# Attention with a mixture-of-experts layer: an early product for values and logits, a third subtraction on ScalarE, and paired score and value steps

## The reference

```python
xn = layernorm(x)                      # x: (8, 512, 128), float32
# attention, 16 heads of 8 channels
q, k, v = split(xn @ w_attn)           # w_attn: (128, 384)
mask = causal - log1p(softplus(decay)[h] * log1p(distance))
att = softmax(q @ k.T / sqrt(8) + mask)
attn = (att @ v) @ w_proj
# mixture of 8 experts, hidden 512, the best two by router logits
logits = xn @ Wr.T
gate = weights of the top 2 of softmax(logits), normalised
ffn = sum over the two of gate * (W2[e] @ silu(W1[e] @ xn))
out = x + attn + ffn
```

## Time and profile before

| | us |
|---|---|
| median of three runs | 574.65 (573.76 to 575.19) |
| the profiled execution | 580.15 |
| its span | 578.4 |
| PE busy | 517.7 (90%) |
| POOL busy | 371.5 (64%) |
| DVE busy | 352.7 (61%) |
| ACT busy | 320.7 (55%) |

### The profile page before, as it was taken

The page is one execution under the profiler, slowest core; times in us unless marked ns, Lnnn a source line. Parts: engine busy times, 40 slices in busy tenths (PEclk is TensorE's granted clock), DMA queues, the critical chain, the costliest instruction groups (busy, mean ns, idle before and its releaser), DMA issues.

```text
span 578.4 us, 13697 instructions
## 1 busy us (share of the span) xinstructions
PE 517.7 (90%) x4472; PEld 370.1 (64%) x4472; DVE 352.7 (61%) x1418; ACT 320.7 (55%) x569; POOL 371.5 (64%) x610
## 2 busy tenths in 40 slices
PE   3589999999999989999999989989999999999930
PEld 1477565565555555565555555545699999999930
DVE  5875898779866766776776676666133333333326
ACT  3656776767776666766776677556523333233300
POOL 3354576467787888788678888888245455554434
PEclk9757999999999999999999999999999999999975
DMA  6553673331430350350241243044546666766439
GB/s 164 164 176 104 189 153 110 111 103 46 134 89 15 121 159 15 98 174 20 83 143 46 70 126 105 16 148 117 134 135 203 210 194 203 221 197 202 145 122 326
DMA packets 69715, 76.49 MB, mean 132 GB/s; under 512 B 8318, under 2 KB 52352, under 8 KB 69648
## 3 DMA queue, kind: packets, MB, share of 16 engines
q1 hardware_dynamic: 65328, 67.16, 39.7%
q0 software_dynamic: 4320, 8.47, 4.3%
HBM read 46.16 MB, written 29.89 MB: 131 GB/s over the span
## 4 chain that ended last, share of the span: by engine, by line
PE 69%; POOL 15%; DVE 6%; issue 3%; DMA 3%; ACT 1%; SPq 1%; another core or an unknown queue 0%; DVEq 0%; POOLq 0%
PE psT L1176 20%; PE ps L1224 11%; PE psT L1251 11%; PE psO L1190 10%; POOL scores L671 8%; POOL rows_dram L682 7%; PE ps L1152 6%; DVE scores L1013 3%; PE psM L1129 3%; PE psM L1082 2%; PE psO L1101 2%; PE psM L1208 1%; DVE x_all L489 1%; PE ps L1215 1%; PE psM L1135 1%
## 5 line engine op out<-in xcount | busy, mean ns | idle before, releaser
L1013 DVE CUSTOM_DVE_ANT_0 scores<-ps,wdist 128x256 f32<-128x256 f32 (+3 forms) x512 | 222.2, 486 | 92.1 <-PE ps L1152 66.3
L671 POOL TENSOR_SCALAR scores<-scores,row_max 128x384 f32<-128x384 f32 (+2 forms) x448 | 221.5, 509 | 77.2 <-DVE row_max L1013 76.0
L776 ACT ACTIVATE probs<-psT 128x512 f32<-128x512 f32 x320 | 175.5, 596 | 80.8 <-PE psT L1176 78.5
L1176 PE MATMUL psT<-ident,scores 128*128 128x128 f32 x1280 | 179.3, 282 | 16.8 <-POOL scores L671 10.9
L1176 PEld LDWEIGHTS psT<-ident,scores 128*128 128x128 f32 x1280 | 138.3, 142 | 57.0 <-POOL scores L671 28.3
L689 POOL DMA_INDIRECT picked_dram<-scores,row_ring x71 | 69.7, 982 | 79.1 <-issue 42.9
L1190 PE MATMUL psO<-probs,values 128*32 128x512 f32 (+3 forms) x1024 | 94.9, 444 | 0.0
L794 ACT ACTIVATE scores<-ps 128x512 f32<-128x512 f32 x71 | 42.4, 597 | 94.1 <-PE ps L1224 94.1
L1224 PE MATMUL ps<-scores,wdist 128*128 128x128 f32 x568 | 75.2, 275 | 1.6 <-issue 1.0
L1251 PE MATMUL psT<-wdist,scores 128*128 x568 | 75.2, 275 | 0.3 <-ACT scores L794 0.3
L682 POOL DMA_INDIRECT rows_dram<-xn_all x64 | 62.8, 981 | 16.2 <-issue 16.2
(11 more groups left out here) (130 smaller groups left out, 322.9 us busy)
## 6 DMA issues: line engine op xcount, KB each, us to landing
wdist<-w1t SPq DMA_DIRECT2D x71, 256.0 KB
k_rows<-k_dram SPq DMA_DIRECT2D x64, 96.0 KB, 3.0
q_rows<-q_dram SPq DMA_DIRECT2D x64, 96.0 KB, 2.5
row_ring<-rows_dram SPq DMA_DIRECT2D x71, 65.0 KB
probs<-picked_dram SPq DMA_DIRECT2D x8, 512.0 KB, 6.8
rows_dram<-row_ring SPq DMA_DIRECT2D x7, 585.0 KB, 5.4
k_dram<-k_parts SPq DMA_DIRECT2D x8, 384.0 KB
q_dram<-q_parts SPq DMA_DIRECT2D x8, 384.0 KB
```

Of the source, the lines that this page charges most:

```text
L671: last = nc.gpsimd.tensor_scalar(part, part, -1.0, row_max[:, r, tile, quad:quad + 1], ALU.mult, ALU.add)
L776: nc.scalar.activation(probs[:, at.ring(2), w, :], psT[:, w % 2], ACT.Exp, scale=-1.0).then_inc(exp_ready, 1)
L1013: last = nc.vector.tensor_tensor_reduce(out=scores[:, r, u, col:col + n], in0=bank[:, col:col + n], in1=wdist[:, at.g * QUADS + quad, SEQ ...
L1176: last = nc.tensor.transpose(psT[:, w % 2, place * P:(place + 1) * P], scores[:, at.ring(2), u, col + key * P:col + (key + 1) * P], ident[:])
```

## The change

The values product and the logits product become one, 136 columns wide (`VL`), for every batch in the prologue and slots 0 and 1. Its result goes half through `psO` and ACT, half through `psM` and DVE, into a staging place; POOL copies the logits out of it (`LC`), SP stores the values of batches 1 to 7 to DRAM (`VS`) and reads them back once per batch (`VR`), and ACT spreads them into `values` (`V`). Unit 6 is subtracted by ACT instead of POOL. In a slot P1 0 and 1, P1 2 and 3, PV 0 and 1, and PV 2 and 3 stand next to each other. The sends stand behind P1 4 and start in slot 8 instead of 10; routing takes slots 2 to 8 instead of 2 to 9 (its last two steps stay in 11 and 12). The normalising of batches 1 to 3 goes to POOL (`NP`), the statistics of the last four batches are split into four steps, the first batch's key and query parts are written for 32 of 128 rows first, and PE gets 18 and 16 matmuls of the identity with itself in the prologue (`WU`).

```diff
@@ -71,24 +71,25 @@
 P1_TILES = (((0, 3),), ((0, 2), (384, 0)), ((0, 1), (256, 1)), ((0, 3),), ((0, 2), (384, 0)))
 DVE_BATCHES, POOL_BATCHES = (0, 1, 3, 4, 6, 7), (2, 5)
 
-ROUTE = {2: {0: ("R1",), 3: ("R2",)},
-         3: {0: ("R3",), 3: ("R4",)},
-         4: {0: ("R5",), 3: ("R6",)},
-         5: {0: ("R7", "GX"), 3: ("R8",)},
-         6: {0: ("CT",), 3: ("R9",)},
-         7: {0: ("R10",), 3: ("R11",)},
-         8: {0: ("R12",), 3: ("R13",)},
-         9: {0: ("R14",), 3: ("R15",)},
+ROUTE = {2: {0: ("R1",), 1: ("R2",), 3: ("R3",)},
+         3: {0: ("R4",), 1: ("R5",), 3: ("R6",)},
+         4: {0: ("R7", "GX"), 1: ("CT",), 3: ("R8",)},
+         5: {0: ("R9",), 3: ("R10",)},
+         6: {0: ("R11",), 3: ("R12",)},
+         7: {0: ("R13",), 3: ("R14",)},
+         8: {0: ("R15",)},
          11: {0: ("R16",)},
          12: {0: ("R17",)}}
-FIRST_SEND_SLOT = 10
+FIRST_SEND_SLOT = 8
 ALL_UNITS = UNITS * NGROUP
 TOPK = 2
-EARLY = {1: (("XB", 8), ("XS", 8), ("XB", 12), ("XS", 12), ("LN", 8), ("LN", 9), ("NX", 16)),
-         2: (("XB", 16), ("XS", 16), ("LG", 8), ("LN", 10), ("LN", 11), ("CZ", 2), ("NX", 20)),
-         3: (("XB", 20), ("XS", 20), ("LG", 12), ("LN", 12), ("LN", 13), ("NX", 24)),
-         4: (("XB", 24), ("XS", 24), ("LG", 16), ("LN", 14), ("LN", 15), ("CZ", 3), ("NX", 28))}
-EARLY_1 = (("XB", 28), ("XS", 28), ("LG", 20), ("LG", 24), ("LG", 28))
+EARLY = {0: (("VL", 12), ("LN", 4), ("LN", 5)),
+         1: (("NX", 16), ("VS", 12), ("LC", 4), ("LN", 6), ("LN", 7), ("CZ", 1)),
+         2: (("XB", 16), ("XS", 16), ("NX", 20), ("LC", 8), ("LN", 8), ("LN", 9)),
+         3: (("VL", 16), ("XB", 20), ("XS", 20), ("VS", 16), ("NX", 24), ("LC", 12), ("LN", 10), ("LN", 11), ("CZ", 2)),
+         4: (("VL", 20), ("XB", 24), ("XS", 24), ("VS", 20), ("NX", 28), ("LC", 16), ("LN", 12), ("LN", 13))}
+EARLY_1 = (("VL", 24), ("XB", 28), ("XS", 28), ("VS", 24), ("LC", 20), ("LN", 14), ("LN", 15), ("CZ", 3), ("VL", 28),
+           ("VS", 28), ("LC", 24), ("LC", 28))
 SENDS = 3
 SECOND_PICK_SLOT = FIRST_SEND_SLOT + -(-NTILE // SENDS)
 
@@ -99,10 +100,13 @@
 TOKEN_ROW = 1 + ROW
 NOWHERE = 1 << 20
 
+WIDE = C + EXPERTS
+POOL_NORMS = (1, 2, 3)
 NORM_PARTS = (slice(0, TILES), slice(TILES, 4 * TILES), slice(4 * TILES, NTILE))
 VCOL = HD + 1
 VROW = HEADS * VCOL + QROWS - VCOL + 1
-ACT_UNITS = 2
+ACT_UNITS = (0, 1, 6)
+POOL_UNITS = tuple(u for u in range(UNITS) if u not in ACT_UNITS)
 FILLS = 8
 PICKS_STEP, GAP_STEP = 12, 13
 TWO23 = 8388608.0
@@ -159,18 +163,19 @@
     step("KD", n + 1, NGROUP)
     step("QD", n + 1, NGROUP)
     p1(0)
+    p1(1)
     step("TE", n - 1, NGROUP, 0, 2)
     per_batch("KA", -3)
     per_batch("QA", -2)
+    per_batch("VR", -2)
     per_batch("V", -1)
     per_batch("YT", 8)
-    step("SA", n, NGROUP)
+    step("SA", n, NGROUP, (0, 1))
     step("PV", n - 2, NGROUP, 0)
-    p1(1)
+    step("PV", n - 2, NGROUP, 1)
     per_batch("KR", -3)
     per_batch("QR", -2)
     step("TE", n - 1, NGROUP, 2, 4)
-    step("PV", n - 2, NGROUP, 1)
     per_batch("KM", -3)
     per_batch("QM", -2)
     if n == NGROUP + 4:
@@ -183,25 +188,26 @@
                 steps.append(("MU", 0, s + 1))
     if n == SECOND_PICK_SLOT:
         steps.append(("SR", 0))
-    pick = int(n > SECOND_PICK_SLOT)
-    first = SENDS * (n - (SECOND_PICK_SLOT + 1 if pick else FIRST_SEND_SLOT))
-    if 0 <= first < NTILE:
-        steps.append(("SC", 0, pick, first, min(NTILE, first + SENDS)))
     if n < FILLS:
         steps.append(("FL", 0, n))
     p1(2)
+    p1(3)
     step("TE", n - 1, NGROUP, 4, 6)
-    step("PV", n - 2, NGROUP, 2)
     per_batch("KL", -3)
     per_batch("QL", -2)
-    p1(3)
+    step("PV", n - 2, NGROUP, 2)
+    step("PV", n - 2, NGROUP, 3)
     step("TE", n - 1, NGROUP, 6, 8)
-    step("PV", n - 2, NGROUP, 3)
     per_batch("KW", -3)
     per_batch("QW", -2)
     per_batch("XT", -4)
     p1(4)
     step("TE", n - 1, NGROUP, 8, 10)
+    step("SA", n, NGROUP, (6,))
+    pick = int(n > SECOND_PICK_SLOT)
+    first = SENDS * (n - (SECOND_PICK_SLOT + 1 if pick else FIRST_SEND_SLOT))
+    if 0 <= first < NTILE:
+        steps.append(("SC", 0, pick, first, min(NTILE, first + SENDS)))
     if n == NGROUP + 2:
         steps.append(("MU", 0, 0))
     step("NT", n - 3, NGROUP)
@@ -213,13 +219,15 @@
 
 
 PROLOGUE = [
-    ("BN", 0, 0), ("RS", 0, 0), ("NX", 0), ("XB", 0), ("KA", 0), ("QA", 0),
-    ("BN", 0, 1), ("RS", 0, 1),
-    ("KR", 0), ("QR", 0), ("KM", 0), ("QM", 0), ("LN", 0), ("LN", 1), ("LN", 2), ("LN", 3), ("CZ", 0),
-    ("KL", 0), ("QL", 0), ("KW", 0), ("QW", 0), ("KD", 0), ("QD", 0),
-    ("NX", 4), ("NX", 8), ("NX", 12), ("BN", 0, 2), ("RS", 0, 2),
-    ("V", 0), ("XB", 4), ("LG", 0), ("LG", 4), ("LN", 4), ("LN", 5), ("LN", 6), ("LN", 7), ("CZ", 1)]
-MISC_KINDS = ("KA", "QA", "V", "NT", "YT", "PJ", "CT")
+    ("BN", 0, 0, 0, 4), ("RS", 0, 0), ("NX", 0), ("WU", 18), ("XB", 0), ("KA", 0), ("QA", 0), ("WU", 16),
+    ("BN", 0, 1, 4, 16), ("RS", 0, 1), ("NP", 4), ("NP", 8), ("NP", 12),
+    ("KR", 0), ("QR", 0), ("KM", 0), ("QM", 0), ("LN", 0), ("LN", 1),
+    ("KL", 0), ("QL", 0), ("KW", 0, 0), ("QW", 0, 0), ("KD", 0), ("QD", 0), ("KW", 0, 1), ("QW", 0, 1),
+    ("VL", 0), ("XB", 4), ("LN", 2), ("LN", 3), ("CZ", 0),
...
 
+        def v_stage(b):
+
+            flat = (probs[:, 0].rearrange("p u k -> p (u k)")[:, b * TILES * WIDE:(b + 1) * TILES * WIDE] if b < 6 else
+                    o_rows[:].rearrange("p r k -> p (r k)")[:, 0:TILES * WIDE] if b == 6 else
+                    y[:].rearrange("p r t c -> p (r t c)")[:, 0:TILES * WIDE])
+            return flat.rearrange("p (t k) -> p t k", k=WIDE)
+
...
+                def values_store(at):
+                    b = at.c // GROUPS
+                    wait_staged(sp, b)
+                    sp.dma_start(v_dram[b - 1], v_stage(b).rearrange("p t k -> p (t k)")
+                                 ).then_inc(v_stored[max(0, b - 5)], 16)
+
+                def values_load(at):
+                    if at.c == GROUPS:
+                        wait_v_stored(sp, True)
+                    else:
+                        sp.wait_ge(values_ready, at.batches(1))
+                    sp.dma_start(v_back[:].rearrange("p t k -> p (t k)"),
+                                 v_dram[bass.ds(at.batches(1, -1), 1)].rearrange("b p s -> p (b s)")
+                                 ).then_inc(v_loaded, 16)
...
 
+                def normalise_step(at):
+                    b = at.c // GROUPS
+                    pool.wait_ge(rstd_ready, 2)
+                    for t in range(b * TILES, (b + 1) * TILES):
+                        last = nc.gpsimd.tensor_scalar(xn_all[:, t, 3:], x_all[:, t, :], mean[:, t:t + 1],
+                                                       rstd[:, t:t + 1], ALU.subtract, ALU.mult)
+                    last.then_inc(xn_pool, 1)
+
+                def logits_step(at):
+                    b = at.c // GROUPS
+                    wait_staged(pool, b)
+                    nc.gpsimd.tensor_copy(logits[:].rearrange("p (t e) -> p t e", e=EXPERTS)[:, b * TILES:(b + 1) * TILES, :],
+                                          v_stage(b)[:, :, C:]).then_inc(logits_ready, 1)
+
                 def causal_step(at):
...
-                        return
                     r = at.ring(2)
                     for strip in range(2):
                         u = 2 * i + strip
+                        if u in ACT_UNITS:
+                            continue
...
-                        nc.scalar.activation(logits[:], psO[:, 0:NTILE * EXPERTS], ACT.Copy).then_inc(logits_ready, 1)
+                def wide_copy(at):
+
+                    act.wait_ge(misc_full, at.misc("VL", 1))
+                    nc.scalar.activation(v_stage(at.c // GROUPS)[:, 0:2, :],
+                                         psO[:, 0:2 * WIDE].rearrange("p (t k) -> p t k", k=WIDE), ACT.Copy
+                                         ).then_inc(vo_free, 1)
+
...
-                def less_act_step(at):
+                def less_act_step(at, units):
 
                     r = at.ring(2)
-                    for u in range(ACT_UNITS):
+                    for u in units:
                         act.wait_ge(p1_free, at.groups(UNITS, u + 1))
-                        part = scores[:, r, u, :]
-                        nc.scalar.activation(part, part, ACT.Identity, scale=-1.0, bias=row_max[:, r, TILES - 1, u:u + 1]
-                                             ).then_inc(less_act, 1)
-
...
 
                 def v_step(at):
-                    act.wait_ge(misc_full, at.misc("V", 1))
+                    act.wait_ge(v_loaded, at.batches(16))
+                    act.wait_ge(pv_full, at.groups(1, -GROUPS))
                     nc.scalar.activation(value_cols[:, at.parity, :, :, 0:HD],
-                                         psM[:].rearrange("p (t h d) -> p t h d", t=TILES, h=HEADS),
-                                         ACT.Copy).then_inc(misc_free, 1)
```

(42 more changed lines are left out.)

127 lines of the change are left out of this document (89 added, 38 removed), and 3 rows, old and new, of the table PROLOGUE.

## The result

The median after is 538.99 us (four runs, 538.42 to 540.09), against 574.37 (573.76 to 575.19) of the kernel before in the same job. The ratio is 0.9385, with a 95% interval of 0.9366 to 0.9405: 35.4 us faster. The forecast was 536.3. The profiled execution took 539.08 us, with a span of 537.4 and a mean granted clock of 0.98.

A forecast was written before the change was run, and what follows sets the result against it. PE was taken as the bound, busy 90% of the span, with POOL closing the loop in sending slots. Gains of 32.0 (slots 9 to 32), 1.3 (2 to 8) and 5.0 (start) sum to 38.3 us: median 536.3, range 528 to 548.

The forecast's parts named there:

- Fewer runs: All slots: joining two score pairs and two value pairs saves 0.50 us a slot, a plain slot becoming 9.38 us.
- the feared wait of the second score step: Each slot: the second score step might wait for DVE to free step 4's banks, with a margin of 0.2 us.
- rivals C and D: Slots wait for DVE through the pairing: C 16 us back, 552, chance 0.08; D 43 us back, 579, chance 0.03.
- 0.50 less 0.15 for near misses: Each slot: 0.50 us saved by joints, 0.15 charged for small waits on DVE or ACT, ends 0 and 0.6.
- The values product: Slots 3, 7, ... 27: V leaves PE's chain, 0.89 us seven times, 6.2 us.
- Sends: Slots 9 to 32: sends at the slot's end, 0.7 us less POOL work; stage 246.0 us, gain 32.0 in all.
- rival A: Sending slots stay bound by POOL and DVE: 13 us come back, 549 us; chance 0.13.
- More important is what waits for the sends: Sending slots: only the next slot's first subtraction waits for moved sends, 2 us or more to spare, so sending waits go.
- Routing brought forward: Slots 2 to 8: three routing parts crowd DVE in slots 2, 3 and 5, 5.5 us of waits; net gain 1.3.
- Prologue: Start, slots 0 and 1: first turn pair near 42, slot 2 near 51 instead of 56.02; gain 5 us, ends 0 and 8.
- the gaps of slot 0: Slot 0: PE's long gaps would drop the clock again after the added matmuls; half clock counted in slots 0 and 1.
- I carry the difference over unchanged: Whole kernel: the profiled execution's 5.5 us over the median (580.15 against 574.65) was taken to stay after the change.

The follow-up runs named there:

- u_unpaired: The changed kernel with score steps and value chunks apart again, in the order of the kernel before: 549.61 us, ratio 0.958.
- p_both: The kernel before with score steps and value chunks in pairs and the sends at the slot's end: 557.66 us, ratio 0.972.
- c_before: The kernel before, unedited, profiled again: 573.60 us, ratio 0.999.
- p_sends: The kernel before with only the sends moved behind the last score step of their slot: 564.02 us, ratio 0.984.
- p_pairs: The kernel before with only score steps and value chunks put in pairs: 556.12 us, ratio 0.969.
- u_nowarm: The changed kernel without the 34 added matmuls of the identity: 541.65 us, ratio 0.943.
- u_sends_mid: The changed kernel with the sends back between the second and third score step: 541.33 us, ratio 0.943.
- u_pool6: The changed kernel with unit 6 subtracted by POOL again instead of ACT: 548.79 us, ratio 0.957.
- u_route10: The changed kernel with routing in slots 2 to 9 and sends from slot 10, as before: 543.05 us, ratio 0.944.
- best_a: The changed kernel with ACT's psO copy after the fourth turn pair's exponentials, routing in two parts over slots 2 to 9, sends from slot 9: 539.38 us.
- best_b: best_a with POOL normalising two batches instead of three and the last statistics ahead of the wide products: 538.07 us, ratio 0.937.

## Why the prediction was right, and where it was not

**Fewer runs: right.** The joints of the value pairs are as computed (2 x 0.14), the score pairs give 0.11 each, and in slots 9 to 32 PE waits 0.3 us in all for DVE's row maxima, so the feared wait of the second score step is absent; rivals C and D fall. What came back is the 0.12 of the last turn pair. The net is 0.38 a slot, near "0.50 less 0.15 for near misses", but the near miss is another than the one named, ACT and not DVE. The fifth turn pair needs the banks that ACT's exponentials of the fourth read. ACT's timeline there, in the changed kernel and in u_unpaired:
```profile
197.58 1.09 ACT L874 ACTIVATE probs<-psT 128x512 f32<-128x512 f32 x2
```
```profile
212.30 1.09 ACT L874 ACTIVATE probs<-psT 128x512 f32<-128x512 f32 x2 [0.62 <-PE psT L1293]
```
The first of the two ends at 198.18 in the changed kernel, and the last pair starts at 198.32; in each of the 32 slots the distance is 0.14 us, for the second window too. In u_unpaired the fourth value chunk (0.57) stands between the two pairs besides the score step, the first exponential ends at 212.89, and the last pair starts 0.63 later: it waits for nothing and takes 1.02.

**The values product: right.** p_both, which keeps it, has 248.0 us of PE time in slots 9 to 32 where the changed kernel has 241.8; five products of 0.89 are 4.5 of that, and p_both's half clock at the end of the stage is in the rest. Not foreseen was the projection's 1.09 that became 0.89, 1.2 us in the stage.

**Sends: right in size; the cause named is enough by itself, but so nearly is another.** The stage came to 243.5 against 246.0 forecast, and PE's idle time fell from 17.2 to 1.7; rival A, POOL-bound sending slots, did not come. "More important is what waits for the sends" gave all of it to their move. Of the 14.9 us that PE idles in c_before's stage, the move alone leaves 3.5, 3.2 of them in slot 32, where its tail is, so the mechanism holds. The pairs alone leave 6.7, both 6.0, and the third subtraction alone all of it. In time of the stage that is 11.9 us for the move, 19.2 for the pairs (10.9 of it PE's own time), 18.9 for both, and none for the third subtraction. Taken out of the changed kernel pairs, move and subtraction cost 9.8, 1.6 and 7.9. So the loop of the earlier trace rows can be opened in two places, by a score step more ahead of it or by moving the sends out, and the second opening adds nothing. Once it is open the load of POOL decides, and there the third subtraction is worth 7.9 us.

**The tail of the sends: missed.** That the start of the sends two slots earlier keeps their last landing from the first expert slot was in no term. Undone it costs 2.1 us. In p_sends and p_both, where the sends run into slot 32 too, that slot is 3.2 and 3.7 us longer than in c_before and p_pairs.

**Routing brought forward: right in kind, priced too high.** 2.5 us were gained in slots 2 to 8 against 1.3 forecast: PE idles 2.5 us there, where 5.5 of waits were charged. DVE is on the chain in slots 2, 3 and 5, as named there, and in 7.

**Prologue: right in kind, 1.4 us too hopeful.** Slot 2 begins at 52.40, forecast 51, and the first turn pair at 43.08, forecast 42. Its parts were further off. The chain of the start shows POOL's normalising and a late first score step:
```profile
15.68 4.97 POOL xn_all L724 x7
...
26.06 2.94 POOL rstd L717
...
42.75 0.33 PE ps L1268 x4
43.08 0.60 PE psT L1293 x4
```
DVE's first score step came at 25.93, not 23.6. What made up for part of it was the clock, which the sum had at half throughout slots 0 and 1. The same view as for the stages, cut where the granted clock changes, answers to the earlier trace rows:
```profile
7.00:31.00 24.00, 16.03 (x114) 12.41 (x114) 17.24 (x72) 12.91 (x24) 18.16 (x22) 1.00 0.68 197
31.00:34.40 3.40, 3.25 (x14) 2.42 (x14) 3.40 (x15) 1.82 (x3) 2.83 (x8) 0.50 0.86 269
34.40:51.06 16.66, 12.01 (x90) 8.45 (x90) 12.80 (x48) 14.50 (x26) 8.99 (x21) 1.00 0.52 175
```
The clock is full (2.4 GHz) behind the first added matmuls, which start at 2.75, and half for only 3.4 us. In u_nowarm it first rises at 20.7, and the matmuls are worth 1 to 3 us. The Trainium skill (TensorE: Matmul & The Clock Gate, "What's actually happening") has sustained activity release the throttle and idling restore it. The first half agrees with the two rises. The second half, by which the prediction expected the gaps of slot 0 to drop the clock, shows as one short fall, although PE was busy only 16.0 of the 24 us ahead of it. Some of that is the execution: u_sends_mid, with the same start, and u_pool6, with nearly the same, fall to half twice, for 10.2 us in all, and reach their first value product 0.7 and 1.0 us later.

**The level: the carried-over difference was wrong.** "I carry the difference over unchanged" took 5.5 us as something that the change leaves alone. By c_before, whose profiled execution is 6.8 us shorter, 5.2 of the 6.8 lay in the stage of the sending slots of that one execution, as waits and as PE time. The changed kernel's execution does not show it, so the changed kernel's profile stands on its median (539.08 and 538.99). The span fell by 41.0 and the median by 35.4. The forecast gain of 38.3 lies between the two, 2.7 below the one and 2.9 above the other, and the forecast time is 2.7 us low. So its nearness is in part luck: the excess of the profiled execution, counted as staying, and the gains, counted too small by 2.7 in sum, err in opposite directions.

## What to carry to other kernels

When a blocking step stands in a loop over several engines, find the whole loop on the chain before pricing an edit: it opens by moving the step out or by giving the loop one more piece of work in advance, and both together give the gain once. Less work on an engine of the loop that is not in the loop's stretch changes nothing before it is open and may be worth much after. Where spread work is moved to the end of its slots, look at what waits for its last piece, and take a second profile of the kernel before when its execution stands a per cent above the median.

## What the runs showed of the hardware

- In the chain of waits a change from one kind of PE work to another costs 0.11 to 0.14 us: 1.00 + 0.78 became 1.64, 0.36 + 0.57 became 0.79, 0.32 + 0.33 became 0.54. Which kind stands ahead matters too: the same projection takes 1.09 behind a value product and 0.89 behind a turn.
- POOL normalises a 128x128 tile with two per-partition operands in 0.78 us (twelve in 9.38), DVE in 0.28 to 0.44. The prediction counted on POOL being out of the way there.
- An indirect send lands 2.3 us after its issue starts (2.35 in p_sends, 2.32 in u_route10, 2.27 in p_both) where the DMA share is 0.17 to 0.18, that is 1.3 to 1.4 after the 0.96 of the issue, but 3.54 in slot 18 of u_pool6, where the share is 0.87. Over all 64 sends the median is 2.7 (best_a, best_b, u_nowarm). The prediction took 1 us after the issue.
- A turn starts 0.14 us after the exponential that it waits for has ended, in each of the 32 slots of the changed kernel.
